# The causal mask of twelve attention groups: a TensorE product into the transposed scores, or a GpSimd selection of the exponentials

## The chip, the cores and the metric

One core of a Trainium2 chip. The metric is the device time of one execution, in microseconds (us), as the median of several runs. The kernel is one program that runs five engines side by side: TensorE (PE in the profile, its weight loads PEld), VectorE (DVE), ScalarE (ACT), GpSimd (POOL) and the queue that issues most transfers (SP).

## The reference, cut to what matters

Four layers over x of 1024 tokens by 256 features, each x + attention(norm(x)) + feed-forward(norm(x)). Layer 0 has a latent attention with 16 heads (rotary and plain features) and beside it a second attention over a shared key; layer 2 has a plain one with 16 heads. All three are causal, and the part that matters here is the same in each:

```python
scores = jnp.einsum('bhtd,bhsd->bhts', q, k) * scale       # layer 0 also adds the rotary product
causal = jnp.tril(jnp.ones((t, t), dtype=bool))
scores = jnp.where(causal[None, None], scores, jnp.float32(-jnp.inf))
attn = jax.nn.softmax(scores, axis=-1)
out = jnp.einsum('bhts,bhsd->bhtd', attn, v)
```

Layer 1 has one causal head over 1024 tokens, layer 3 a running sum in place of attention. The layers' other halves are gated products and aren't touched.

## The kernel before, in words

Heads are taken in 12 groups of four (`GH`): groups 0, 2, 4, 6 are the latent ones of layer 0 (`is_mla`), 1, 3, 5, 7 the ones with a shared key (`is_shared`), 8 to 11 those of layer 2. `GROUPS` holds the two runs, 0 to 7 and 8 to 11. Each group walks over the 8 key tiles (`kt`, 128 keys each).

**Scores (`score_units`, `scores_T`, L1956 to L1985).** For a key tile the scores are computed transposed: 128 keys on the partitions, queries along the columns, from the key tile's first query (`kt * P`) to 1024, in products of at most 512 columns. For kt 0 to 3 a unit is one head in two halves; for kt 4 to 7 it is two heads, one half each. A latent group needs two products for each half: L1962 (`Kr2`, `Qr2`, 128 rows) and L1963 (`Kr`, `Qr`, 113 rows), both 4-byte. The other groups need only L1963, 97 rows of bf16 parts. The last row of the stacks adds minus the row maximum. Each unit goes into one of two halves of `psA` (`a_unit` waits until ScalarE has read the unit before last).

**Exponentials (L1100, L1105).** ScalarE reads each unit out of `psA` through Exp into `Pr` and counts `a_drained`. `Pr` holds two key tiles (places s % 2).

**Selections (`mask_exponentials`, L930 to L936).** When all units of a key tile are drained, GpSimd sets to zero, in place, what lies above the diagonal in the 128 x 128 block of each of the four heads, in one instruction over 512 columns, and counts `masked`.

**Values (`values_product`, L1987 to L2004).** TensorE waits for `masked`, and multiplies the exponentials by the values into `psO`, four heads side by side in 32-column strips. It runs one key tile behind the scores: it is issued after the second unit (and, for kt 0 to 3, the third) of the next key tile (L2098).

**Maxima (`maxima_unit`, L1930 to L1948; VectorE L1420).** The row maxima of the next group are found from untransposed scores in `psD` (two banks; `d_unit` waits until VectorE has read the unit before last). These already carry a mask: behind a product whose block holds the diagonal comes `identb` x `maskq` into its last 128 columns (L1947). When all are reduced, VectorE forms the negated maxima, TensorE transposes them (L1953), and a transfer puts them into the stack as the row of the next group.

**The order of TensorE's work.** It is written by a planner, `paced` with its class `Pace` (L117 to L209): it keeps a clock for each engine in TensorE columns, and after each score unit or values product it takes as many waiting units (maxima, rotary products, selected keys, down weights) as find a free bank, or as the share of the group that has passed asks for. Two of its costs concern the change: `points_of` (the columns of a score unit) and `MASKED`, 1900, after which a key tile's exponentials count as ready for the values product; `HANDOVER` is 480.

**GpSimd's other work between the selections** (L953 to L966): rotary sums, splits of a query tile into bf16 parts, eight-way butterflies of a weight in group 6, and in the last group low parts of expert weights (L1010).

**`scores_T` already has a `mask` argument**, which the layer-1 attention uses (L2275): in the diagonal half it adds `identb` x `maskk` to the first 128 columns (L1965), where `maskk` is 0 where the query may see the key and -1e30 elsewhere, in bf16.

Of the kernel before, what the change touches and what calls it, by code (L numbers as in the profile page):

```python
# [7 lines left out]
ALU = mybir.AluOpType  # L8
# [3 lines left out]
P = 128  # L12
T, D = 1024, 256
NT, DC = T // P, D // P
HALF = 512
H, HD, RD, LAT = 16, 16, 64, 64
GH = 4
# [56 lines left out]
def is_mla(i):  # L74

    return i < 2 * NG and i % 2 == 0
# [34 lines left out]


READ, EXPONENTIAL = (368, 2.5), (400, 2)
MASKED, HANDOVER, SHORT = 1900, 480, 600


class Pace:  # L117


    def __init__(self):  # L120
        self.pe = self.dve = self.act = 0
        self.read, self.copied, self.masked = [0, 0], [0, 0], {}

    def bank_free(self):
        return self.read[-2] <= self.pe + SHORT
# [9 lines left out]
        self.copied.append(self.act)  # L135

    def values(self, columns, s):
        self.pe = max(self.pe, self.masked[s]) + columns


def points_of(groups, i, kt):

    heads = GH if kt < NT // 2 else GH // 2
    points = []
    for k in range(heads):
        points.append(("scores", (T - kt * P) * (1 if kt < NT // 2 else 2) * (2 if is_mla(i) else 1)))
        if (i, kt) != (groups[0], 0) and k in (1, 2):
            columns, b = 0, (kt - 1) % NT
            for half in (0, 1) if heads == 2 else (k - 1,):
                if b * P < (half + 1) * HALF:  # L150
                    columns += HANDOVER + 4 * ((half + 1) * HALF - max(b * P, half * HALF))
            points.append(("values", columns))
    return points


def paced(groups):

    pace, plan, waiting, due, passed = Pace(), {}, {}, {}, {}
    for g in groups[1:]:
        waiting[g], passed[g] = list(MAX_UNITS), 0  # L160
        due[g] = sum(columns for place in max_window(g, groups[0]) for _, columns in points_of(groups, *place))

    def maxima(j, part, h0, nh, w):
        pace.unit(nh * w + (nh * P if part == (j >= NT // 2) else 0), nh * w)

    for i in groups:
        for kt in range(NT):
            g = next((g for g in (i + 1, i + 2) if g in groups and (i, kt) in max_window(g, groups[0])), None)
            products = beside_products(i, kt)
            row = i + 1 in groups and kt == max_end(i + 1)  # L170
            points = points_of(groups, i, kt)
            if (i, kt) == (0, KEY_KT):
                pace.pe += 8 * T
            if (i, kt) == (2 * NG - 1, NT // 2 - 1):
                pace.pe += 8 * T
            plan[i, kt] = (g, [])
            for n, (what, columns) in enumerate(points):
                if what == "scores":
                    pace.scores(columns, (T - kt * P) * (1 if kt < NT // 2 else 2))
                else:  # L180
                    pace.values(columns, NT * i + kt - 1)
                if row and n == 1:
                    pace.pe = max(pace.pe, pace.read[-1] + 2 * HANDOVER)
                    pace.unit(4 * P, P)
                at = []
                behind = 0
                if g is not None:
                    passed[g] += columns
                    behind = len(waiting[g]) - len(MAX_UNITS) * (due[g] - passed[g]) // due[g]
                while (products or waiting.get(g)) and not (row and n == 0):  # L190
                    if not pace.bank_free() and (n < len(points) - 1 if products else len(at) >= behind):
                        break
                    at.append(products.pop(0) if products else waiting[g].pop(0))
                    if at[-1][0] == "rope":
                        pace.unit(2 * HALF, HALF)
                    elif at[-1][0] == "wdn":
                        pace.unit(4 * HALF, HALF, 2)
                    elif at[-1][0] == "kv":
                        pace.unit(8 * HALF, 3 * HALF, 2)
                    else:  # L200
                        maxima(*at[-1])
                plan[i, kt][1].append(at)
            pace.masked[NT * i + kt] = pace.act + MASKED
            if kt == 1 and i - 1 in groups:
                for _ in range(2):
                    pace.unit(16 * P, HALF + (0 if is_mla(i - 1) else 2 * HALF), 2)
            if i == 2 * NG - 1 and kt >= NT // 2:
                pace.unit(8 * HALF, HALF)
    return plan  # L209
# [11 lines left out]
def build(nc, ins, out):  # L221
    with ExitStack() as ctx:
# [380 lines left out]
        stack_in = [sem(f"stack_in{n}") for n in range(4)]  # L603
        part0_cut, keys_masked, head_ready = sem("part0_cut"), sem("keys_masked"), sem("head_ready")
        max_ready, mrow_in = sem("max_ready"), sem("mrow_in")
        pv_done, masked = sem("pv_done"), sem("masked")
        butterflies, had_ready, ones1_ready = sem("butterflies"), sem("had_ready"), sem("ones1_ready")
        se_args, se_ready, comb_ready, comb_out = (
            sem(n) for n in ("se_args", "se_ready", "comb_ready", "comb_out"))
# [234 lines left out]
        def _(pool):  # L844
# [82 lines left out]
            nope_rest(1)  # L927
            nope_rest(3)

            def mask_exponentials(i, kt):  # L930

                s = NT * i + kt
                pool.wait_ge(a_drained, scored(i, kt))
                block_ = Pr[:, (s % 2) * GH * T:(s % 2 + 1) * GH * T].rearrange("p (h t) -> p h t", h=GH)[:, :, tile_cols(kt)]
                pool.affine_select(out=block_, in_=block_, pattern=[[0, GH], [1, P]], compare_op=ALU.is_ge, fill=0.0,  # L935
                                   base=0, channel_multiplier=-1).then_inc(masked, 1)  # L936

            STEPS_AT = (0, 4, 8, 12, 13, 14, 14, 14, 14)  # L940
            steps_1 = [(s, q, op) for s in range(3) for q in range(0, FC, 2 << s) for op in (ALU.add, ALU.subtract)]

# [9 lines left out]

            for i in GROUPS[0]:  # L953
                for kt in range(NT):
                    mask_exponentials(i, kt)
                    if (i, kt) in ROPE_AT:
                        rope_add(ROPE_AT[i, kt])
                    if (i, kt - 1) in ROPE_AT:
                        rope_rest(ROPE_AT[i, kt - 1])
                    if i == 1 and kt < 4:  # L960
                        split_step(1, kt)
                    if i == 6:
                        if kt == 0:
                            pool.wait_ge(w1_in, 16 * N_W1)
                        for step in steps_1[STEPS_AT[kt]:STEPS_AT[kt + 1]]:
                            butterfly(*step)  # L966
# [39 lines left out]

            for i in GROUPS[2]:
                for kt in range(NT):
                    mask_exponentials(i, kt)
                    if i == LAST and kt in (1, 2, 3):  # L1010
                        piece_low(kt - 1)
            for e in range(E):
# [823 lines left out]
        def _(pe):  # L1836
# [131 lines left out]
            def score_units(i, kt):  # L1968

                rows = MLA_ONE + 1 if is_mla(i) else STACK + 1  # L1970

                def one(heads):
                    dst = a_unit()
                    for b, h in enumerate(heads):
                        second = (Kr2[:, tile_cols(kt)], lambda lo, hi: Qr2[:, h * T + lo:h * T + hi]) if is_mla(i) else None
                        k = key_rows(i, h, rows, kt * P, (kt + 1) * P)
                        q = lambda lo, hi: head_rows(Qs, i, h, rows, lo, hi)
                        if len(heads) == 1:
                            for half in range(2):
                                op = scores_T(dst, half * HALF, k, q, kt, half, second)  # L1980
                        else:
                            op = scores_T(dst, b * HALF, k, q, kt, 1, second)
                    op.then_inc(a_filled, 1)
                step = 1 if kt < NT // 2 else 2
                return [list(range(h, h + step)) for h in range(0, GH, step)], one  # L1985

            def values_product(i, kt, halves):  # L1987

                s = NT * i + kt
                pe.wait_ge(masked, s + 1)  # L1990
                if kt == 0 and i > 0:
                    pe.wait_ge(o_drained, i)
                for half in halves:
                    if kt * P >= (half + 1) * HALF:
                        continue
                    lo, hi = max(kt * P, half * HALF), (half + 1) * HALF
                    last_kt = hi // P - 1
                    for h in range(GH):
                        e = Pr[:, ((s % 2) * GH + h) * T + lo:((s % 2) * GH + h) * T + hi]
                        op = pe.matmul(psO[h * VW:(h + 1) * VW, lo:hi], values(i, kt, h), e,  # L2000
                                       start=kt == 0, stop=kt == last_kt, tile_position=(0, h * VW),
                                       skip_group_check=True)
                if 1 in halves:
                    op.then_inc(pv_done, 1)  # L2004
# [467 lines left out]
```

## Time and profile before

| | |
|---|---|
| median of 3 runs | 916.07 us (912.64 to 919.23) |
| the profiled execution: time, span | 915.74 us, 914.0 us |
| busy: TensorE products, VectorE, ScalarE, GpSimd | 824.8, 563.4, 388.4, 238.4 us |
| mean granted TensorE clock | 0.967 of 2.4 GHz |
| selections: number, busy | 96, 61.0 us |

The profile is of one execution. Products of TensorE are pipelined, and their recorded durations include that pipeline, so the busy time of TensorE is more than the time it needs. "The chain of waits" follows the work that ended last back from the end: at each step to what released it, or to the instruction before it on its engine. A releaser is inferred; "issue" is time in which an engine waited for nothing that is recorded. Idle time of an engine counts only where the chain passes.

### The profile page before, as it was taken

How to read it: one execution, taken by the hardware profiler on the slowest of the kernel's cores; microseconds unless marked ns; L12 is line 12 of the kernel's file. 1: busy time of each engine (PE TensorE's matmuls, PEld its weight loads, DVE VectorE, ACT ScalarE, POOL GpSimd, SP SyncE). 2: the span in 40 equal slices, each digit the busy share in tenths (PEclk: the TensorE clock that was granted, in tenths of full speed). 3: DMA queues.
4: the chain of work that ended last, by engine and by line, in shares of the span. 5: the costliest groups of instructions: out<-in, count | busy, mean ns of one | idle time of the engine just before them, and what ended most of it. 6: DMA issues, size and time to landing. Idle time of an engine off the chain costs nothing.

```text
span 914.0 us, 12060 instructions
## 1 busy us (share of the span) xinstructions
PE 824.8 (90%) x4833; PEld 491.4 (54%) x4835; DVE 563.4 (62%) x1000; ACT 388.4 (42%) x481; POOL 238.4 (26%) x215
## 2 busy tenths in 40 slices
PE   8989999899899999996899997858999889989997
PEld 3554553454355435444478793523343248888776
DVE  4987657784876678216543454848776545965552
ACT  3731454446444545563423403134554854510240
POOL 4641222421132114513322101501111236720110
PEclk9989999999999999998989998979999999999999
DMA  6473169416532850204000003779000052000001
GB/s 190 87 245 72 47 146 145 116 47 110 99 82 79 135 141 1 79 1 141 22 1 1 1 1 130 146 120 118 2 2 1 3 195 94 0 1 1 1 0 47
DMA packets 35585, 64.99 MB, mean 71 GB/s; under 512 B 6165, under 2 KB 14909, under 8 KB 35461
## 3 DMA queue, kind: packets, MB, share of 16 engines
q1 hardware_dynamic: 34952, 64.08, 30.1%
q8 instruction: 38, 0.62, 0.3%
q10 hardware_dynamic: 576, 0.13, 0.1%
q14 instruction: 19, 0.15, 0.1%
HBM read 44.35 MB, written 16.29 MB: 66 GB/s over the span
## 4 chain that ended last, share of the span: by engine, by line
PE 66%; DVE 18%; ACT 6%; issue 3%; SPq 3%; POOL 2%; DMA 2%; ACTq 0%; DVEq 0%; POOLq 0%
PE psD L1860 12%; PE psO L2000 11%; PE psA L1860 10%; PE psD L1945 9%; PE psA L1963 8%; DVE mx L1420 8%; PE psO L1860 7%; PE psA L1962 3%; SPq L627 3%; ACT Pr L1100 2%; PE psD L1947 2%; DVE hid_low L1756 1%; PE psD L2014 1%; PE psA L1893 1%; DVE Qs L1541 1%
## 5 line engine op out<-in xcount | busy, mean ns | idle before, releaser
L1420 DVE TENSOR_REDUCE mx<-psD 128x1 f32<-128x512 f32 (+3 forms) x419 | 259.3, 657 | 95.8 <-PE psD L1947 70.5
L1100 ACT ACTIVATE Pr<-psA 128x1024 f32<-128x1024 f32 (+3 forms) x192 | 161.7, 865 | 174.7 <-PE psA L1963 174.3
L935 POOL TENSOR_SCALAR_AFFINE_SELECT Pr<-Pr 128x512 f32<-128x512 f32 x96 | 61.0, 635 | 372.1 <-ACT Pr L1100 296.6
L1105 ACT ACTIVATE Pr<-psA 128x1024 f32<-128x1024 f32 (+3 forms) x96 | 63.6, 703 | 59.9 <-PE psA L1963 59.7
L2000 PE MATMUL psO<-Pr,Vh 128*32 128x512 f32 (+3 forms) x768 | 80.8, 500 | 3.1 <-POOL Pr L935 2.6
L1962 PE MATMUL psA<-Qr,Kr 128*128 128x512 f32 (+3 forms) x192 | 74.7, 403 | 0.7 <-ACT xnT L1045 0.7
L1947 PE MATMUL psD<-maskq,identb 128*128 128x128 bf16 x354 | 70.5, 224 | 0.1
L1963 PE MATMUL psA<-Qr,Kr 113*128 113x512 f32 (+3 forms) x192 | 65.5, 347 | 0.0
L1945 PE MATMUL psD<-Kg,Qs 96*128 96x512 bf16 (+3 forms) x192 | 54.5, 332 | 7.8 <-DVE mx L1420 4.9
L1963 PE MATMUL psA<-Qs,Ks 97*128 97x512 bf16 (+3 forms) x192 | 46.3, 334 | 12.3 <-issue 8.3
L1945 PE MATMUL psD<-Kr,Qr 80*128 80x512 bf16 (+3 forms) x166 | 50.8, 348 | 7.0 <-DVE mx L1420 6.1
L1963 PE MATMUL psA<-Qs,Kg 97*128 97x512 bf16 (+3 forms) x192 | 44.5, 326 | 3.5 <-ACT Pr L1100 1.5
L1962 PEld LDWEIGHTS psA<-Qr,Kr 128*128 128x128 f32 x192 | 36.6, 191 | 18.1 <-ACT Pr L1105 8.4
L1945 PE MATMUL psD<-Ks,Qs 96*128 96x512 bf16 (+3 forms) x144 | 42.8, 342 | 3.6 <-DVE mx L1420 2.8
L1945 PEld LDWEIGHTS psD<-Kg,Qs 96*128 96x128 bf16 x192 | 17.7, 97 | 52.5 <-DVE mx L1420 38.9
L1945 PEld LDWEIGHTS psD<-Kr,Qr 80*128 80x128 bf16 x166 | 16.3, 101 | 45.6 <-DVE mx L1420 37.9
L2000 PE MATMUL psO<-Pr,Vg 128*32 128x512 f32 (+3 forms) x384 | 40.1, 497 | 0.7 <-POOL Pr L935 0.2
L1963 PEld LDWEIGHTS psA<-Qr,Kr 113*128 113x128 f32 x192 | 36.6, 190 | 2.9 <-issue 0.7
L1947 PEld LDWEIGHTS psD<-maskq,identb 128*128 128x128 bf16 x354 | 35.5, 100 | 4.4 <-issue 1.5
L1945 PEld LDWEIGHTS psD<-Ks,Qs 96*128 96x128 bf16 x144 | 13.8, 100 | 39.5 <-DVE mx L1420 34.3
L1534 DVE TENSOR_TENSOR x<-x,psD 128x512 f32<-128x512 f32 x11 | 7.6, 687 | 43.3 <-PE psD L1860 35.9
L1963 PEld LDWEIGHTS psA<-Qs,Ks 97*128 97x128 bf16 x192 | 15.3, 100 | 33.4 <-issue 11.4
(433 smaller groups left out, 1696.3 us busy)
## 6 DMA issues: line engine op xcount, KB each, us to landing
Qr<-d_qr SPq DMA_DIRECT2D x18, 512.0 KB, 12.3
d_qr<-WB SPq DMA_DIRECT2D x9, 512.0 KB, 3.2
Pr<-d_cb SPq DMA_DIRECT2D x8, 512.0 KB, 7.7
Qs<-d_gq SPq DMA_DIRECT2D x24, 128.0 KB, 4.1
Qs<-d_q SPq DMA_DIRECT2D x24, 128.0 KB
Ks<-d_k SPq DMA_DIRECT2D x24, 128.0 KB
Qr<-d_qn SPq DMA_DIRECT2D x18, 128.0 KB, 7.3
Kr<-d_kn SPq DMA_DIRECT2D x18, 128.0 KB, 7.9
```

What stands on the lines that cost most here:

```text
L627: sp.dma_start(dst, src).then_inc(s, 16)
L935: pool.affine_select(out=block_, in_=block_, pattern=[[0, GH], [1, P]], compare_op=ALU.is_ge, fill=0.0, base=0, channel_multiplier=-1).the ...
L1100: act.activation(place[:, h, q0:T], src[:, q0:T], ACT.Exp, scale=score_scale(i)).then_inc(a_drained, 1)
L1105: act.activation(place[:, h:h + 2, q0:T], src[:, :, q0 - HALF:HALF], ACT.Exp, scale=score_scale(i)).then_inc(a_drained, 1)
L1420: dve.tensor_reduce(mx[:, j, part, h0:h0 + nh], src, AX, ALU.max).then_inc(d_drained, 1)
L1541: dve.tensor_tensor(dst[:, c], src[0:r, :], gate_rows[:, c], ALU.mult).then_inc(d_drained, 1)
L1860: op = pe.matmul(dst, lhsT, rhs, start=start and k == 0, stop=stop and k == len(terms) - 1)
L1945: op = pe.matmul(dst[:, k * w:(k + 1) * w], q, kk, start=True, stop=not diagonal)
L1947: op = pe.matmul(dst[:, (k + 1) * w - P:(k + 1) * w], identb[:], maskq[:], start=False, stop=True)
L1962: pe.matmul(out_, second[0], second[1](lo, (half + 1) * HALF), start=True, stop=False)
L1963: op = pe.matmul(out_, k, q(lo, (half + 1) * HALF), start=second is None, stop=not (diagonal and mask))
L2000: op = pe.matmul(psO[h * VW:(h + 1) * VW, lo:hi], values(i, kt, h), e, start=kt == 0, stop=kt == last_kt, tile_position=(0, h * VW), skip_ ...
```

## The change

GpSimd's selections and their semaphore go. `scores_T` is called with `mask=True` in the twelve groups, so that each diagonal half gets a product more (L1965). The values product waits for ScalarE's last exponential of the key tile in place of the selection. The planner counts the columns of the mask products, and takes exponentials as ready `HANDOVER` after ScalarE.

```diff
@@ -111,7 +111,7 @@
 
 
 READ, EXPONENTIAL = (368, 2.5), (400, 2)
-MASKED, HANDOVER, SHORT = 1900, 480, 600
+HANDOVER, SHORT = 480, 600
 
 
 class Pace:
@@ -119,7 +119,7 @@
 
     def __init__(self):
         self.pe = self.dve = self.act = 0
-        self.read, self.copied, self.masked = [0, 0], [0, 0], {}
+        self.read, self.copied, self.ready = [0, 0], [0, 0], {}
 
     def bank_free(self):
         return self.read[-2] <= self.pe + SHORT
@@ -135,7 +135,7 @@
         self.copied.append(self.act)
 
     def values(self, columns, s):
-        self.pe = max(self.pe, self.masked[s]) + columns
+        self.pe = max(self.pe, self.ready[s]) + columns
 
 
 def points_of(groups, i, kt):
@@ -143,7 +143,7 @@
     heads = GH if kt < NT // 2 else GH // 2
     points = []
     for k in range(heads):
-        points.append(("scores", (T - kt * P) * (1 if kt < NT // 2 else 2) * (2 if is_mla(i) else 1)))
+        points.append(("scores", ((T - kt * P) * (2 if is_mla(i) else 1) + P) * (1 if kt < NT // 2 else 2)))
         if (i, kt) != (groups[0], 0) and k in (1, 2):
             columns, b = 0, (kt - 1) % NT
             for half in (0, 1) if heads == 2 else (k - 1,):
@@ -200,7 +200,7 @@
                     else:
                         maxima(*at[-1])
                 plan[i, kt][1].append(at)
-            pace.masked[NT * i + kt] = pace.act + MASKED
+            pace.ready[NT * i + kt] = pace.act + HANDOVER
             if kt == 1 and i - 1 in groups:
                 for _ in range(2):
                     pace.unit(16 * P, HALF + (0 if is_mla(i - 1) else 2 * HALF), 2)
@@ -603,7 +603,7 @@
         stack_in = [sem(f"stack_in{n}") for n in range(4)]
         part0_cut, keys_masked, head_ready = sem("part0_cut"), sem("keys_masked"), sem("head_ready")
         max_ready, mrow_in = sem("max_ready"), sem("mrow_in")
-        pv_done, masked = sem("pv_done"), sem("masked")
+        pv_done = sem("pv_done")
         butterflies, had_ready, ones1_ready = sem("butterflies"), sem("had_ready"), sem("ones1_ready")
         se_args, se_ready, comb_ready, comb_out = (
             sem(n) for n in ("se_args", "se_ready", "comb_ready", "comb_out"))
@@ -927,16 +927,6 @@
             nope_rest(1)
             nope_rest(3)
 
-            def mask_exponentials(i, kt):
-
-                s = NT * i + kt
-                pool.wait_ge(a_drained, scored(i, kt))
-                block_ = Pr[:, (s % 2) * GH * T:(s % 2 + 1) * GH * T].rearrange("p (h t) -> p h t", h=GH)[:, :, tile_cols(kt)]
-                pool.affine_select(out=block_, in_=block_, pattern=[[0, GH], [1, P]], compare_op=ALU.is_ge, fill=0.0,
-                                   base=0, channel_multiplier=-1).then_inc(masked, 1)
-
-
-
             STEPS_AT = (0, 4, 8, 12, 13, 14, 14, 14, 14)
             steps_1 = [(s, q, op) for s in range(3) for q in range(0, FC, 2 << s) for op in (ALU.add, ALU.subtract)]
 
@@ -952,7 +942,6 @@
 
             for i in GROUPS[0]:
                 for kt in range(NT):
-                    mask_exponentials(i, kt)
                     if (i, kt) in ROPE_AT:
                         rope_add(ROPE_AT[i, kt])
                     if (i, kt - 1) in ROPE_AT:
@@ -1006,7 +995,6 @@
 
             for i in GROUPS[2]:
                 for kt in range(NT):
-                    mask_exponentials(i, kt)
                     if i == LAST and kt in (1, 2, 3):
                         piece_low(kt - 1)
             for e in range(E):
@@ -1977,9 +1965,9 @@
                         q = lambda lo, hi: head_rows(Qs, i, h, rows, lo, hi)
                         if len(heads) == 1:
                             for half in range(2):
-                                op = scores_T(dst, half * HALF, k, q, kt, half, second)
+                                op = scores_T(dst, half * HALF, k, q, kt, half, second, mask=True)
                         else:
-                            op = scores_T(dst, b * HALF, k, q, kt, 1, second)
+                            op = scores_T(dst, b * HALF, k, q, kt, 1, second, mask=True)
                     op.then_inc(a_filled, 1)
                 step = 1 if kt < NT // 2 else 2
                 return [list(range(h, h + step)) for h in range(0, GH, step)], one
@@ -1987,7 +1975,7 @@
             def values_product(i, kt, halves):
 
                 s = NT * i + kt
-                pe.wait_ge(masked, s + 1)
+                pe.wait_ge(a_drained, scored(i, kt))
                 if kt == 0 and i > 0:
                     pe.wait_ge(o_drained, i)
                 for half in halves:
```

## Rows read from the trace of the kernel before

**Rows 1.** Page, busy us by engine; clock granted in 40 slices

```profile
PE 824.8 (90%) x4833; PEld 491.4 (54%) x4835; DVE 563.4 (62%) x1000; ACT 388.4 (42%) x481; POOL 238.4 (26%) x215
...
PEclk9989999999999999998989998979999999999999
```

**Rows 2.** Timeline, PE: bf16 products of 128 columns behind one another

```profile
145.61 0.22 PE L1945 MATMUL psD<-Kr,Qr 80*128 80x128 bf16 x1
145.67 0.22 PE L1947 MATMUL psD<-maskq,identb 128*128 128x128 bf16 x1
145.73 0.22 PE L1945 MATMUL psD<-Kr,Qr 80*128 80x128 bf16 x1
```

**Rows 3.** Page and chain of waits, shares of the span

```profile
PE 66%; DVE 18%; ACT 6%; issue 3%; SPq 3%; POOL 2%; DMA 2%; ACTq 0%; DVEq 0%; POOLq 0%
...
by line: PE psD L1860 11.6%; PE psO L2000 10.7%; PE psA L1860 10.1%; PE psD L1945 9.2%; PE psA L1963 8.0%; DVE mx L1420 7.6%; PE psO L1860 7.1%; PE psA L1962 3.4%; issue 3.0%; SPq L627 2.6%; ACT Pr L1100 2.0%; PE psD L1947 1.9%; DVE hid_low
```

**Rows 4.** Waits: engine, line waited for, us in total, times, longest

```profile
ACT Pr L1100 <- PE psA L1963: 174.3, 128, 10.0
PEld psD L1945 <- DVE mx L1420: 112.7, 220, 1.9
...
PEld psD L1953 <- DVE mneg L1425: 9.6, 8, 2.6
```

**Rows 5.** Line 935, the selections: number, ns, who waited for them

```profile
L935 POOL TENSOR_SCALAR_AFFINE_SELECT Pr<-Pr x96: 627/634/688, 84.3 to 740.4; 128x512 f32<-128x512 f32 x96
...
  PEld psO L2000: 11.3, 23
  PE psO L2000: 2.8, 7
  PEld psA L1963: 1.3, 1
```

**Rows 6.** Timeline, PE: values products that waited for a selection

```profile
376.37 0.85 PE L2000 MATMUL psO<-Pr,Vh 128*32 128x384 f32 x8 [0.58 <-POOL Pr L935]
...
712.95 0.64 PE L2000 MATMUL psO<-Pr,Vh 128*32 128x256 f32 x8 [0.42 <-POOL Pr L935]
...
741.12 0.43 PE L2000 MATMUL psO<-Pr,Vh 128*32 128x128 f32 x8 [0.83 <-POOL Pr L935]
```

**Rows 7.** Timeline, PE: products of 128 columns with f32 weights

```profile
131.55 0.27 PE L1962 MATMUL psA<-Qr,Kr 128*128 128x128 f32 x1
...
131.66 0.27 PE L1963 MATMUL psA<-Qr,Kr 113*128 113x128 f32 x1
```

**Rows 8.** Chain of waits, pieces in order of time: start us, us, what

```profile
184.11 0.18 PE psA L1962
...
184.47 0.24 PE psA L1962
...
189.20 0.06 PE psD L1947
```

**Rows 9.** Page, the score products: count, busy us, mean ns, idle before

```profile
L1962 PE MATMUL psA<-Qr,Kr 128*128 128x512 f32 (+3 forms) x192 | 74.7, 403 | 0.7 <-ACT xnT L1045 0.7
...
L1963 PE MATMUL psA<-Qr,Kr 113*128 113x512 f32 (+3 forms) x192 | 65.5, 347 | 0.0
...
L1963 PE MATMUL psA<-Qs,Ks 97*128 97x512 bf16 (+3 forms) x192 | 46.3, 334 | 12.3 <-issue 8.3
...
L1963 PE MATMUL psA<-Qs,Kg 97*128 97x512 bf16 (+3 forms) x192 | 44.5, 326 | 3.5 <-ACT Pr L1100 1.5
```

**Rows 10.** Chain of waits, a bf16 group: products of 512 and 256 columns

```profile
147.68 0.33 PE psA L1963 x2
```

**Rows 11.** Groups by line and form, VectorE: busy us, mean ns

```profile
L1420 DVE TENSOR_REDUCE mx<-psD 128x1 f32<-128x512 f32 x262 | 169.8, 685 | 36.2 <-PE psD L1945 21.9 <-PE psD L1947 13.3 <-DVE xn L1450 0.2
...
L1756 DVE TENSOR_TENSOR hid_low<-Qs,hid_high 128x1024 fp32r<-128x1024 f32 x8 | 15.3, 1908 | 0.0
...
L1666 DVE TENSOR_TENSOR hid_low<-Qs,hid_high 128x1024 fp32r<-128x1024 f32 x8 | 9.6, 1217 | 0.0
```

## What the change will do to the time: the prediction

> **What bounds the kernel now.** I read the page's busy table first, then the chain of waits, then the list of waits, then the timeline around single products. The table has TensorE busy 90% of the span, VectorE 62%, GpSimd only 26%, and TensorE's clock at full speed through nearly all of it [rows 1]. Busy TensorE time is padded: a product of 128 columns is written down as 0.22 us while the next starts 0.06 us later [rows 2]. So I take the bound from the chain. It runs 66% over TensorE, 18% over VectorE and 2% over GpSimd; the two lines of the transposed scores hold 8.0% (L1963) and 3.4% (L1962) of it, the maxima reductions of VectorE 7.6% [rows 3]. The attention stages alternate: TensorE fills a bank and goes on; the next bank it wants is still being reduced by VectorE (220 waits, 112.7 us on the weight-load side), and ScalarE waits 174.3 us for score products [rows 4]. The last shows that ScalarE has time to spare and that score products are what it lacks. GpSimd's 96 selections take 0.634 us each, 61 us in all, but TensorE was held by them for only 11.3 + 1.3 us on its load side and 2.8 us on its product side [rows 5]. The engine that is being relieved is thus nearly free, and the work goes to the one that holds most of the chain.
>
> **What is removed.** 96 selections and the wait on them before each values product. The wait that replaces it (last exponential of the same key tile) is met in advance: the values products come behind the second score unit of the next key tile, and that unit could only start once this same exponential had left its bank. So nothing new is late there. Worth: the seven waits in which products really stood still are 2.8 us [rows 5], three of them being 0.58, 0.42 and 0.83 us [rows 6]. A product's record runs 0.22 us where its successor starts after 0.06 [rows 2], so each such gap is really about 0.16 us longer: 2.8 + 7 x 0.16 = 3.9 us. The other 16 or so load-side waits lie below that padding; I allow 0.6 us. Gain 4.5 us. Its ends: 2.8 us from the product side alone, and 11.3 + 2.8 + 1.3 = 15.4 us if every wait of either side were worth its full length.
>
> **What is added.** Each score product of the diagonal half gets one more: 12 groups x 8 key tiles x 4 heads = 384 products of 128 columns, bf16, each with its own load of the identity. The maxima already do exactly this in VectorE's banks: product and mask follow each other at 145.61, 145.67, 145.73 us, that is 0.06 us each, load hidden [rows 2]; a mask on the chain holds the same (189.20) [rows 8]. In the eight groups with bf16 stacks the price is 0.06 us. In the four latent groups the product behind a mask often needs an f32 load. Such products of 128 columns stand 0.11 us apart (131.55, 131.66), where bf16 ones stand 0.06 apart [rows 2, 7]: the f32 load, which a product of 512 columns covered, sticks out from behind a mask. Of a latent group's 32 masks, those followed by L1962 inside their unit (16 in the first four key tiles, 8 in the last four) cost 0.11, except the 4 + 2 whose own product has 128 columns, where the load was already out in the open (0.06). So 18 x 0.11 + 14 x 0.06 = 2.8 us a group, 0.088 us a mask. In all: 4 x 2.8 + 256 x 0.06 = 26.6 us of TensorE time.
>
> **How much of it is on the path.** A chain step that was late stays late, so masks behind products on the chain lengthen it in full; masks that TensorE runs while VectorE is reducing cost nothing. The share follows from time on the chain over time in all. In a latent group the 24 products of 512 columns take 0.24 us, the 8 of 384 0.18 [rows 8], the 8 of 256 about 0.12 (in proportion) and the 8 of 128 0.11 [rows 7]: 9.1 us, 36.3 in four groups. The chain has 3.4% x 914 = 31.1 us of L1962: 86%. L1963 comes in the same 192 latent products and in 2 x 192 of bf16 [rows 9]; 8.0% x 914 = 73.1 us, less 31.1 for the latent ones (same sizes, same places) and some 2 for the layer-1 scores, leaves 40. A 512 and a 256 in bf16 take 0.33 us together [rows 10], so a group has 24 x 0.22 + 8 x 0.17 + 8 x 0.11 + 8 x 0.06 = 8.0 us, eight groups 64: 62%. Masks on the chain: 128 x 0.86 = 110 at 0.088 us = 9.7 us, and 256 x 0.62 = 159 at 0.06 = 9.5 us. Sum 19.2 us. The bounds are none of the bf16 half absorbed or all of it: from 9.7 to 26.6 us.
>
> The Trainium skill (TensorE: Matmul & The Clock Gate, Back-to-back issue gap) says that a stream of load and product pairs of 128 columns sustains about 81 ns each, against this change. An estimate by it is 269 x 0.081 = 22 us on the chain instead of 19.2. The trace's alternating pairs disagree at 0.06 us [rows 2], and I stay with them.
>
> **What moves.** The planner that spreads the maxima over the score units changes two numbers: 128 more columns for each head, and exponentials ready 480 instead of 1900 columns after ScalarE, 0.6 us sooner at 2.4 GHz. Both are small against a unit, so some maxima move by one place. I take 0 for it. What a move can cost or give is read from VectorE: a reduction of 0.685 us [rows 11] finished too late or in time, once in each of 11 hand-overs between groups: 7.5 us either way. GpSimd's other work (rope sums, butterflies, low parts) comes out from behind the selections, but nothing on the chain waits for it apart from what is counted above. VectorE could gain if GpSimd had been in its way: the same 128 x 1024 subtraction takes 1908 ns in one stage and 1217 in another [rows 11], but the reductions, which are the bulk of its attention work, hold 685 ns; I take 0, and bound it at 2 us.
>
> **Sum.** 914.0 - 4.5 + 19.2 = 928.7 us span; the profiled execution took 915.74 us beside it, so 930.4. That execution stands 0.3 below the median of 916.07. I say 930.
>
> **The rivals.**
> A. Not slower: TensorE's slack takes the masks. Place: the 220 waits for VectorE's banks, half a microsecond each [rows 4]. If the new order puts score units, then 0.06 to 0.17 us longer, into these waits, only the latent groups' 9.7 us remain, and with most of the 15.4 us of selection waits coming back (say 9) the time is 915.74 + 9.7 - 9 = 916. Pushed further (a reduction in time at each hand-over, -7.5) it is 909. For it: the slack is there. Against it: 62% of the bf16 score products are on the chain already, in the order of now. It decides from the point at which under a fifth of the masks stay on the path.
> B. Slower by more: the shift of maxima goes the wrong way. The last maxima of a group come late, and TensorE stands before the transposing product (eight waits now, 9.6 us [rows 4]). All 26.6 us count and 7.5 come on top, with the 2.8 us gain: 915.74 + 26.6 + 7.5 - 2.8 = 947. Half of it gives 939.
> C. The change doesn't relieve GpSimd's followers at all, because the seven waits turn into waits for ScalarE: 915.74 + 19.2 = 935. It is inside the forecast's own range.
>
> **How the numbers follow.** Forecast (with C) 0.62, A 0.25, B 0.13. Forecast's own range 922 to 937. The range that leaves out two in ten reaches into A as far as 914 and into B as far as 940. A measurement of this kernel tells about 1% (9.2 us) from no change. Slower by over that, above 925.2: four fifths of the forecast's case, and B: 0.62. Within: the rest of the forecast's case and most of A: 0.28. Faster: the far end of A: 0.10.
>
> **What would show it.** Right: a new group at L1965 with 384 + 8 products, starting 0.06 us behind their product in bf16 groups and followed at 0.11 in latent ones; L935 gone; GpSimd busy near 238 - 61 = 177 us; values products no longer waiting for GpSimd; each group of attention 1 to 2.5 us longer; the chain with about 16 to 20 us of L1965. Wrong: VectorE's share of the chain falling by ten microseconds or more (A), or a wait before the transposing product several microseconds longer (B), or mask products at 0.08 us and over.

## The result, and the profile after

The changed kernel took 927.68 us in the median (922.37 to 928.75, 4 runs) beside 914.36 us for the kernel before (4 runs): ratio 1.0107, 95% interval 1.0064 to 1.015. A second comparison on one chip (8 runs against 25) gave 1.0091, 1.0061 to 1.0121. Slower by 5.6 to 13.7 us, then. The profiled execution is the fastest of its four, with a span of 920.6 us.

The page of the changed kernel: busy times, granted clock, and the shares of the chain.

```profile
PE 850.1 (92%) x5217; PEld 511.8 (56%) x5219; DVE 560.3 (61%) x1000; ACT 390.3 (42%) x481; POOL 177.3 (19%) x119
...
PEclk9989999999999999998889998989999999999999
...
PE 73%; DVE 17%; ACT 5%; issue 2%; DMA 1%; POOL 1%; SPq 0%; DVEq 0%; ACTq 0%; POOLq 0%
...
L1950 PE MATMUL psA<-Qr,Kr 128*128 128x512 f32 (+3 forms) x192 | 84.6, 441 | 0.7 <-ACT xnT L1033 0.7
L1953 PE MATMUL psA<-maskk,identb 128*128 128x128 bf16 x392 | 84.6, 225 | 0.0
```

Against [rows 1] GpSimd has lost 61 us, and TensorE has gained 25. The mask products are there, 392 with the eight of layer 1, at L1953 now. The row to stop at is L1950, the old L1962 [rows 9]: it does the same 192 products, and its busy time has risen from 74.7 to 84.6 us.

The waits of the changed kernel (in total, times, longest), and its chain by line:

```profile
PEld psD L1933 <- DVE mx L1408: 94.1, 196, 1.2
```

```profile
by line: PE psD L1848 11.9%; PE psO L1988 11.2%; PE psA L1848 11.0%; PE psD L1933 10.0%; PE psA L1951 9.4%; DVE mx L1408 7.4%; PE psO L1848 7.1%; PE psA L1950 4.6%; PE psA L1953 2.1%; issue 2.1%; PE psD L1935 2.1%; ACT Pr L1088 1.5%; DVE hi
```

No wait for a selection is left. Those of the values products' loads have become shorter waits for ScalarE, which weren't there before, while the products themselves wait neither for a selection nor for an exponential any more:

```profile
PEld psO L1988 <- ACT Pr L1088: 4.5, 18, 0.4
PEld psO L1988 <- ACT Pr L1093: 4.4, 18, 0.5
```

Waits for VectorE's banks have fallen from 112.7 to 94.1 us [rows 4]; experiments 4, 8 and 9 tell which masks went into them. L1953 holds 2.1% x 920.6 = 19.3 us of the chain.

**A finer ruler.** One execution differs from the next by several microseconds, but not everywhere. VectorE copies out each group's row of maxima once (a cast to `mrowb` in the groups with bf16 stacks, to `mrow` in the latent ones), while the group before it is at its fifth or sixth key tile. In the middle of layer 0 the stretch from one shared group's row to the next one's holds a shared and a latent group's worth of work, 32 masks of each kind. Where the same code was profiled twice, this stretch agreed within 0.1 us. In the kernel before, from group 3's row to group 5's:

```profile
210.49 0.28 DVE L1438 CAST mrowb<-psD 32x128 bf16<-32x128 f32 x1 [3.09 <-PE psD L1953]
...
294.20 0.28 DVE L1438 CAST mrowb<-psD 32x128 bf16<-32x128 f32 x1 [3.09 <-PE psD L1953]
```

and in the changed kernel:

```profile
210.23 0.28 DVE L1426 CAST mrowb<-psD 32x128 bf16<-32x128 f32 x1 [4.36 <-PE psD L1941]
...
296.67 0.28 DVE L1426 CAST mrowb<-psD 32x128 bf16<-32x128 f32 x1 [4.36 <-PE psD L1941]
```

83.71 us before, 86.44 after: a pair of groups costs 2.7 us more. (The second profile of the changed kernel has 86.46; experiment 12, whose code is that of before up to the last group, has 83.69.) This "pair" is the ruler of the experiments. It isn't the same everywhere, so a longer one stands beside it: from group 2's row to group 7's, 204.75 us before and 212.56 after, again within 0.1 us for the same code. TensorE's granted clock is 1.00 in both stretches in every profile.

What differs between executions lies elsewhere: ahead of group 1's row, after attention, from group 10's row to group 11's, where the mean clock of the stretch is between 0.88 and 0.96 (it takes 39.2 us at 0.96 and 40.9 at 0.92 in the two profiles of the changed kernel), and where the first group of layer 2 waits for its row's transfer. There TensorE stood 8.27 us in the profile of before and 4.72 us in that of the change, which is 3.5 us of why the two spans differ by only 6.6:

```profile
607.84 1.01 PE L1963 MATMUL psA<-Qs,Ks 97*128 97x512 bf16 x2 [8.27 <-issue]
```

```profile
611.75 0.58 PE L1951 MATMUL psA<-Qs,Ks 97*128 97x512 bf16 x1 [4.72 <-issue]
```

### The profile page after: what moved, and what is told of

The parts are those of the page before. It is cut to its first block, busy times and chain, and to the rows that moved or that the text cites. A ratio compares the mean times of both kernels' runs of the same rounds, so it can differ in the third digit from the quotient of the medians.

```text
span 920.6 us, 12725 instructions
## 1 busy us (share of the span) xinstructions
PE 850.1 (92%) x5217; PEld 511.8 (56%) x5219; DVE 560.3 (61%) x1000; ACT 390.3 (42%) x481; POOL 177.3 (19%) x119
## 4 chain that ended last, share of the span: by engine, by line
PE 73%; DVE 17%; ACT 5%; issue 2%; DMA 1%; POOL 1%; SPq 0%; DVEq 0%; ACTq 0%; POOLq 0%
PE psD L1848 12%; PE psO L1988 11%; PE psA L1848 11%; PE psD L1933 10%; PE psA L1951 9%; DVE mx L1408 7%; PE psO L1848 7%; PE psA L1950 5%; PE psA L1953 2%; PE psD L1935 2%; ACT Pr L1088 2%; DVE hid_low L1744 1%; PE psD L2002 1%; DVE xn L1368 1%; DVE Qs L1529 1%
## 5 line engine op out<-in xcount | busy, mean ns | idle before, releaser
L1950 PE MATMUL psA<-Qr,Kr 128*128 128x512 f32 (+3 forms) x192 | 84.6, 441 | 0.7 <-ACT xnT L1033 0.7
L1953 PE MATMUL psA<-maskk,identb 128*128 128x128 bf16 x392 | 84.6, 225 | 0.0
L1951 PE MATMUL psA<-Qs,Ks 97*128 97x512 bf16 (+3 forms) x192 | 52.6, 336 | 8.5 <-issue 4.7
L1951 PE MATMUL psA<-Qs,Kg 97*128 97x512 bf16 (+3 forms) x192 | 50.9, 327 | 2.2 <-ACT Pr L1088 1.2
L1953 PEld LDWEIGHTS psA<-maskk,identb 128*128 128x128 bf16 x392 | 38.5, 98 | 23.4 <-issue 15.2
L1950 PEld LDWEIGHTS psA<-Qr,Kr 128*128 128x128 f32 x192 | 37.9, 197 | 16.5 <-ACT Pr L1093 8.4
L1933 PEld LDWEIGHTS psD<-Kr,Qr 80*128 80x128 bf16 x166 | 16.1, 100 | 38.2 <-DVE mx L1408 31.8
L1951 PEld LDWEIGHTS psA<-Qs,Ks 97*128 97x128 bf16 x192 | 18.7, 99 | 31.8 <-ACT Pr L1088 10.3
L993 POOL TENSOR_TENSOR egu_low<-WA,pieces_k 128x512 fp32r<-128x512 f32 x6 | 7.7, 1280 | 136.2 <-ACT pieces_k L1063 136.2
## 6 DMA issues: line engine op xcount, KB each, us to landing
Qr<-d_qr SPq DMA_DIRECT2D x18, 512.0 KB, 11.6
```

What stands on the lines that cost most here:

```text
L1933: op = pe.matmul(dst[:, k * w:(k + 1) * w], q, kk, start=True, stop=not diagonal)
L1950: pe.matmul(out_, second[0], second[1](lo, (half + 1) * HALF), start=True, stop=False)
L1951: op = pe.matmul(out_, k, q(lo, (half + 1) * HALF), start=second is None, stop=not (diagonal and mask))
L1953: op = pe.matmul(out_[:, 0:P], identb[:], maskk[:], start=False, stop=True)
```

## The experiments

My theory: the masks on the chain are the cost (19 us), the selections were worth 4.5, the order nothing. Rivals: the planner's new order is part of it; slack takes the masks; the selections were worth far more.

**1. The change beside its parts.** No edit.

> The changed kernel itself, beside the runs that take it apart, on the same chip. Both theories expect what was measured before: ratio to the kernel before 1.006 to 1.015.

Measured: ratio 1.0091 (1.0061 to 1.0121), 927.14 us against 917.61.

**2. Masks in the order of before.** Edit to the changed kernel:

```diff
-HANDOVER, SHORT = 480, 600
+MASKED, HANDOVER, SHORT = 1900, 480, 600
-        points.append(("scores", ((T - kt * P) * (2 if is_mla(i) else 1) + P) * (1 if kt < NT // 2 else 2)))
+        points.append(("scores", (T - kt * P) * (1 if kt < NT // 2 else 2) * (2 if is_mla(i) else 1)))
-            pace.ready[NT * i + kt] = pace.act + HANDOVER
+            pace.ready[NT * i + kt] = pace.act + MASKED
```

> The change with the planner's two numbers as they were (1900 and no mask columns). My theory (the order moves little, the masks on the chain are the cost): within 2 us of the changed kernel. Rival (the planner's new order is part of the cost, or of what softens it): 4 us or more away from the changed kernel, on either side.

Measured: ratio 1.0139 (1.0105 to 1.0173), 931.78 us. That is 4.6 us slower than the change, at the rival's mark. The pair:

```profile
213.46 0.28 DVE L1426 CAST mrowb<-psD 32x128 bf16<-32x128 f32 x1 [3.50 <-PE psD L1941]
...
301.04 0.28 DVE L1426 CAST mrowb<-psD 32x128 bf16<-32x128 f32 x1 [3.50 <-PE psD L1941]
```

87.58 us, 1.1 more than the change. So the order isn't worth nothing: in the pair the new one takes back a quarter of the 4.0 us that masks cost in the old order. How much it is in all is less sure. The two ratios lie 0.5% apart, with an uncertainty of nearly as much. The longer ruler has 2.3 us less with the new order, the stretch from group 9's row to group 10's 0.4 more, so what can be read of it in the trace is some 2 us.

**3. Neither selections nor masks, order of before.** Experiment 2 with `mask=True` taken out of both calls in `score_units`.

> No selections and no masks, order of before: layers 0 and 2 attend without a causal mask. What it saves against the kernel before is the whole worth of the selections. My theory: 4.5 us (ratio 0.995). Rival (most waits for GpSimd count): 10 us or more (ratio 0.989 or less).

Measured: ratio 0.9955 (0.993 to 0.998), 914.23 us: 4.1 us for all selections, as worked out. The pair is 83.54 us, only 0.2 less than before; little is to be had in the middle. A gain lies where TensorE has no maxima to go on with, as in the last stretch, from the row of group 11 to the last copy of the outputs: 31.8 us before, 30.7 here. In this one profile, though, the granted clock averaged 0.95 there, where it is 1.00 in all others. At 1.00 the stretch takes 30.0 us with neither (experiment 4) and 31.8 with selections (experiment 5), in the order of the change. So the selections are worth 1.8 us there. The interval of all selections is 1.8 to 6.4 us.

**4. Neither, order of the change.**

> No selections and no masks, order of the change (layers 0 and 2 attend without a causal mask). The changed kernel minus this is the cost of 384 mask products in place. My theory: 19 us between the two, so a ratio of about 0.99 to 0.995 to the kernel before. Rival (slack takes half the masks): 10 us or less between the two. Second rival (all count): 26 us.

Measured: ratio 0.9933 (0.9907 to 0.9959), 912.87 us. The masks cost 1.0091 - 0.9933 = 1.6%, or 14.5 us, in the order of the change, and 1.0139 - 0.9955 = 1.8%, or 16.9 us, in the order of before. Forecast 19.2; between the first rival's 10 and my 19. The pair:

```profile
210.46 0.28 DVE L1426 CAST mrowb<-psD 32x128 bf16<-32x128 f32 x1 [3.83 <-PE psD L1941]
...
293.54 0.28 DVE L1426 CAST mrowb<-psD 32x128 bf16<-32x128 f32 x1 [3.83 <-PE psD L1941]
```

83.08 us. All masks of a pair cost 86.45 - 83.08 = 3.4 us, those between the rows of groups 2 and 7 (156 masks) 212.6 - 203.6 = 9.0 us. The 14.5 us for all has an uncertainty of about 4 us.

**5. Selections in the order of the change.** The kernel before with the planner's two lines of the change.

> The kernel before with only the planner's two numbers of the change: selections stay, no masks. The order was worth about 4 us beside masks and 2 us without either. If the order is simply better: 2 to 4 us faster than before (ratio 0.996 to 0.998). Rival (the old 1900 was there for the selections, which the new order puts on the path): 2 us or more slower than before, with the waits for GpSimd up from 11.3 us.

Measured: ratio 1.0019 (0.9992 to 1.0047). The pair is 83.16 us, 0.5 less, and the longer ruler 1.0 less, but from group 9's row to group 10's it is 0.5 more; the waits for GpSimd are as they were (11.4 us), and the median doesn't show a gain. The rival fails by its own mark, and the forecast of 2 to 4 us faster does too: alone, the order isn't worth a measurable amount.

**6. Each mask twice.** `for again in range(2)` around the mask product in the twelve groups.

> The change with each mask product of the twelve groups issued twice (384 more products, same result). If a mask costs a fixed share of its 0.06 to 0.11 us (the chain in series): another 23 us of TensorE time (the second one always stands 0.06 behind the first), of which 60 to 75% shows: 14 to 17 us over the change, like the first set. Rival (the first set used up the slack in VectorE's waits): the second set shows in nearly full, 20 us or more.

Measured: ratio 1.0311 (1.0284 to 1.0339), 942.56 us: 20 us over the change by the ratios, 15 by the medians, which come from two chips. The two don't agree well enough to choose between the two expectations. The pair is 88.56 us, another 2.1 for 64 x 0.06 = 3.8 us of products (55%), and the longer ruler 218.10, another 5.5 for 156 x 0.06 = 9.4 us (59%), which speaks for the first in layer 0: the first set had not used up the slack there.

**7. Masks behind the unit.** In `score_units` the mask products of a unit come after its last score product.

```diff
-                if diagonal and mask:
+                if diagonal and late is not None:
+                    late.append(out_[:, 0:P])
+                elif diagonal and mask:
                     op = pe.matmul(out_[:, 0:P], identb[:], maskk[:], start=False, stop=True)
...
+                    for out_ in late:
+                        op = pe.matmul(out_, identb[:], maskk[:], start=False, stop=True)
                     op.then_inc(a_filled, 1)
```

> The change with the mask products of a unit put behind the unit's last score product, so that none stands ahead of an f32 load inside the unit. My theory (18 masks of each latent group pay 0.05 us for that load): 0.9 us less in each latent group, 3.6 us in all, and nothing in the bf16 groups. Rival (the load isn't what costs, the masks' own time is): within 1 us of the change in the latent groups too.

Measured: ratio 1.0101 (1.0067 to 1.0135), which can't be told from the change. The pair is 85.50 us, 0.95 less, as expected in size. That it comes from the latent group follows from elsewhere: the layer-2 stretches, which have bf16 masks only, don't change (34.19 for 34.24, 31.1 for 31.2), and the busy time of L1950 falls from 84.6 back to 75.9 us. The longer ruler is 2.9 us shorter, too much for the rival. What it shows besides is the price of one mask inside a unit. The chain of the changed kernel, start and us of each piece:

```profile
184.90 0.18 PE psA L1950
185.08 0.18 PE psA L1951
185.26 0.07 PE psA L1953
185.34 0.32 PE psA L1950
185.65 0.24 PE psA L1951
```

and with the masks behind the unit:

```profile
184.46 0.17 PE psA L1950
184.63 0.18 PE psA L1951
184.81 0.24 PE psA L1950
185.05 0.24 PE psA L1951
185.29 0.07 PE psA L1974
```

A product of 512 columns takes 0.24 us, as in [rows 8]. Behind a mask it takes 0.32 (0.29 in most places). With its own 0.07 such a mask costs 0.12 to 0.15 us, not the 0.11 of my sum. This is where L1950's busy time came from. The weight loads (PEld) of the kernel before and of the changed one show what the product waits for:

```profile
184.13 0.19 PEld L1962 LDWEIGHTS psA<-Qr,Kr 128*128 128x128 f32 x1
...
185.10 0.10 PEld L1953 LDWEIGHTS psA<-maskk,identb 128*128 128x128 bf16 x1 [0.17 <-issue]
185.10 0.20 PEld L1950 LDWEIGHTS psA<-Qr,Kr 128*128 128x128 f32 x1
```

Before, this load of 0.19 us ran beside the product of 384 columns ahead of it, which started at 184.13 too and holds 0.18 us. After, the load starts with the mask product (185.10), which holds only 0.07. The price stood in the trace of before as well, where a maxima mask comes ahead of a latent group's score product:

```profile
339.85 0.06 PE psD L1947
339.91 0.29 PE psA L1962
```

**8. Masks in the latent groups only.** `mask=is_mla(i)` in both calls.

> Order of the change, no selections, masks in the four latent groups only (the other eight attend without a causal mask). Against the kernel with neither it shows the latent groups' part of the 14.5 us that all masks cost. My theory (chain share 86% at 0.088 us against 62% at 0.06): half of it, 7 to 9 us, some 2.2 us in each latent group. Rival (masks cost the same anywhere): a third of it, 5 us.

Measured: ratio 1.0082 (1.005 to 1.0115). The pair:

```profile
210.19 0.28 DVE L1426 CAST mrowb<-psD 32x128 bf16<-32x128 f32 x1 [4.36 <-PE psD L1941]
...
296.16 0.28 DVE L1426 CAST mrowb<-psD 32x128 bf16<-32x128 f32 x1 [4.36 <-PE psD L1941]
```

85.97 us. The latent group's 32 masks cost 2.9 of the 3.4 us; I expected 2.2. By the ratios it is 1.0082 - 0.9933 = 1.5%, more than my 7 to 9 us, but this difference has an uncertainty of 4 us, and four times 2.9 is 11.6. Not every latent group pays the same: from group 5's row to group 7's the same masks cost 80.11 - 76.46 = 3.65 us. On the longer ruler 84 latent masks cost 8.2 us, 0.098 us each.

**9. Masks in the bf16 groups only.** `mask=not is_mla(i)`.

> Order of the change, no selections, masks in the eight bf16 groups only (the four latent ones attend without a causal mask). Stretches between row hand-overs repeat to 0.1 us, and by them a latent and a shared group together take 83.1 us with no mask, 86.0 with latent masks only, 86.45 with all. If the two kinds add up (bf16 masks of layer 0 are mostly absorbed beside VectorE): 83.4 to 83.8 us, a quarter of their 1.9 us. Rival (the first masks to come are absorbed, whichever they are, and the slack is shared): 82.9 to 83.2, nothing at all. My prediction's share of 62% would be 84.3.

Measured: ratio 0.9998 (0.9965 to 1.003). The pair:

```profile
208.25 0.28 DVE L1426 CAST mrowb<-psD 32x128 bf16<-32x128 f32 x1 [3.84 <-PE psD L1941]
...
291.85 0.28 DVE L1426 CAST mrowb<-psD 32x128 bf16<-32x128 f32 x1 [3.82 <-PE psD L1941]
```

83.60 us, 0.5 for the shared group's 32 masks, a quarter of their 1.9 us. 0.5 and 2.9 make the 3.4 of both: the two kinds add up, and the rival of a shared slack falls. On the longer ruler 72 shared masks cost 1.1 us, which with the 8.2 is within 0.4 of the 9.0 of both. The slack is VectorE's, as its waits over the whole kernel show: with neither kind (experiment 4), with the bf16 masks only, and with the latent masks only (experiment 8):

```profile
PEld psD L1933 <- DVE mx L1408: 113.2, 232, 1.7
...
PEld psD L1933 <- DVE mx L1408: 96.9, 203, 1.1
...
PEld psD L1933 <- DVE mx L1408: 109.9, 224, 1.4
```

The bf16 masks, 256 x 0.06 = 15.4 us of products, take 16.3 us off these waits, the latent ones 3.3. In layer 2 the same bf16 masks cost more: the stretch from the row of group 9 to that of group 10 takes 33.2 us without masks and 34.2 with them, half of their 1.9 us, and the last stretch 30.0 and 31.2, half of the 2.4 us of its 40 masks.

**10 and 11. One planner number at a time**, each a single execution.

> The change, with only one of the planner's numbers new: exponentials ready after 480, mask columns not counted. The pair of a latent and a shared group took 87.5 us with both numbers old and 86.45 with both new. If readiness is what helps: 86.5. If the columns are: 87.5.

> The change, with only the other number new: mask columns counted, exponentials ready after 1900. If the columns are what helps: 86.5 us for the pair. If readiness is: 87.5.

Measured: the pair takes 87.66 us with only the readiness new and 86.47 with only the columns. The columns are what helps; the 1900 of the selections did no harm. The waits of the weight loads for VectorE's banks sum to 93.7 us in experiment 1 and in experiment 2 alike. But those of the products themselves, in which TensorE really stood still, are fewer and shorter with the new placing of the maxima. In experiment 2 and in experiment 1:

```profile
PE psD L1933 <- DVE mx L1408: 11.0, 27, 0.9
...
PE psD L1933 <- DVE mx L1408: 7.1, 19, 0.6
```

They are 11.6 us with only the readiness new and 7.1 with only the columns. So the placing helps by bringing fewer products to a bank that is still being reduced.

**12. TensorE masks in the last group only**, selections elsewhere, order of before:

```diff
-                pe.wait_ge(masked, s + 1)
+                if i == LAST:
+                    pe.wait_ge(a_drained, scored(i, kt))
+                else:
+                    pe.wait_ge(masked, s + 1)
```

with `mask=i == LAST` in both calls, and no selection in that group.

> The kernel before, with TensorE masks in place of the selections in the last group alone, where TensorE stood longest for GpSimd and ScalarE holds the chain. The last stretch takes 31.8 us before, 31.2 with masks, 30.7 with neither. Expected: 0.6 us less in that stretch, paid with up to 1 us at the group's start where maxima don't fill it; total within the measurement of the kernel before (0.997 to 1.001). Rival (GpSimd's waits at the end are worth their length, 4 to 5 us in the last group): ratio 0.995.

Measured: ratio 0.9979 (0.9956 to 1.0002), 915.04 us against 917.05. The loads' waits for GpSimd fall from 11.3 to 6.8 us, and the last stretch from 31.8 to 31.4 us:

```profile
PEld psO L2004 <- POOL Pr L935: 6.8, 17, 0.8
```

4.5 us of waits away, 0.4 us of time back in that stretch. This is a balance: by experiments 4, 5 and 9 the selections were worth 1.8 us there and the masks cost 1.2. That 1.8 is near the 2.0 us of the product side's five waits in that stretch and far from the 5.4 us of the load side's. It may be the best of the versions that compute the whole layer, but the interval reaches 1, so that isn't shown.

**All stretches.** In us, from one profile each (two for the change), between the rows of the groups named; "last" is from group 11's row to the last copy of the outputs.

| kernel | row 3 to 5 (pair) | row 2 to 7 | row 9 to 10 | last |
|---|---|---|---|---|
| before | 83.71 | 204.75 | 32.73 | 31.8 |
| the change | 86.44, 86.46 | 212.56, 212.57 | 34.24, 34.23 | 31.2, 31.2 |
| 2, masks, order of before | 87.58 | 214.91 | 33.84 | 31.2 |
| 3, neither, order of before | 83.54 | 204.38 | 32.72 | 30.7 (clock 0.95) |
| 4, neither, order of the change | 83.08 | 203.57 | 33.23 | 30.0 |
| 5, selections, order of the change | 83.16 | 203.74 | 33.23 | 31.8 |
| 6, each mask twice | 88.56 | 218.10 | 35.40 | 32.5 |
| 7, masks behind the unit | 85.50 | 209.64 | 34.19 | 31.1 |
| 8, latent masks only | 85.97 | 211.76 | 33.24 | 30.0 |
| 9, bf16 masks only | 83.60 | 204.71 | 34.24 | 31.2 |
| 10, only the readiness new | 87.66 | 215.04 | 33.84 | 31.2 |
| 11, only the columns new | 86.47 | 212.64 | 34.24 | 31.2 |
| 12, masks in the last group | 83.69 | 204.64 | 32.73 | 31.4 |

## Why the prediction was right, and where its terms were off

The sum said 930, and the comparisons give 8 to 13 us slower for its 14.7. What bounds the kernel and what the change trades were right. That the sum came so near is in part luck: the two terms of the masks were off in opposite directions, and the order was put at nothing.

- **The selections' worth (4.5 us): right.** Experiment 3 measures 4.1 (1.8 to 6.4); 1.8 of it lies in the last stretch, 0.4 between the rows of groups 2 and 7, and the rest wasn't located. The wait list of 15 us would have misled; the seven waits of the product side [rows 5] were the right ones to count.
- **The bound: right.** GpSimd's busy time fell by 61 us as forecast (177 us), and the kernel became slower.
- **The latent masks (9.7 us): the mechanism right, the price too small.** I took 0.11 us for a mask ahead of an f32 load, from products of 128 columns that follow each other [rows 7]. It is 0.12 to 0.15 (experiment 7). Experiment 8 has 2.9 us in one pair and 3.65 in the next where I had 0.86 x 2.8 = 2.4, and 8.2 us on the longer ruler where my terms give 84 x 0.86 x 0.088 = 6.4. The share of 86% was too low as well.
- **The bf16 masks (9.5 us): the share was too large for layer 0.** The chain held 62% of these score products by my count, but their masks cost a quarter in the shared groups and half in layer 2 (experiment 9). On the longer ruler that is 1.1 us where my terms give 72 x 0.62 x 0.06 = 2.7. Both kinds together come to 9.0 us there, and my terms to 9.0 too: 1.8 us too little for one kind and 1.5 too much for the other. I had one average over eight groups, which differ by two. The likely reason, by the waits of experiment 9, is that the mask behind a product on the old chain can take the place of a wait for VectorE, so it needn't cost its time. Why the shared groups absorb more than those of layer 2 was not traced further and stays open.
- **The order (0 us): wrong, by 2 to 4.6 us.** Experiments 2, 10 and 11: the planner's mask columns save 1.1 us in the pair and 2.3 on the longer ruler, and lose 0.4 in layer 2; the medians say 4.6, with an uncertainty of about 4. I had bounded it at 7.5 us either way and taken the middle. With it the sum is 10 to 12.7 us. The lower end lies in both measured intervals, the upper only in that of the first comparison (to 13.7; the second ends at 11.1).
- **The chain after.** It holds 19.3 us of mask products, just what I forecast, yet the masks cost 14.5. The agreement is of two different things (the 14.5 has an uncertainty of 4 us, so the gap is near it): the chain after the change runs through the masks, and past other pieces of the old one (VectorE 17% for 18%). What a new piece holds in the chain afterwards isn't what it cost.
- **The rivals.** A had its mechanism: the waits for VectorE fell by 18.6 us, and the bf16 masks are what went into them (experiment 9), but the latent ones, at nearly full price, kept it from deciding. B did not come: the waits before the transposing product fell, from 9.6 to 6.5 us on the load side. VectorE's own wait for that product grew by 1.3 us (4.36 for 3.09 in the rows above). C came in its mechanism only: the loads' waits for GpSimd became 8.9 us of waits for ScalarE, so the replacing wait wasn't always met in advance, but no product waited for an exponential, and the selections' 4.1 us were had all the same.
- The Trainium skill's 81 ns for a pair of load and product (TensorE: Matmul & The Clock Gate, Back-to-back issue gap) isn't borne out for bf16 masks: on the chain a mask holds 0.06 to 0.07 us. Its rule there that the spacing is set by both operations, the load and the product, fits the f32 loads: 0.29 to 0.32 us behind a mask in place of 0.24.

## What to carry to other kernels

Moving work off an engine that is 26% busy onto the one that holds two thirds of the chain pays only what the waits on the idle engine really held up, here 4 us of 61, and it costs the new work's price in each stage by that stage's own slack: here nearly in full in the latent groups (8.2 us for 84 masks), a half in layer 2 and a quarter in the shared groups. Price a small product with its successor: if the next one loads f32 weights, those come out from behind it. Count the new work in whatever plans the order; that alone gave back a quarter of the masks' cost in the stretches that can be read. And find a stretch of the trace that repeats to 0.1 us from one execution to the next, since it resolves what medians that scatter by 1% can't. Look at its granted clock first, and measure more than one such stretch: the same masks cost 2.9 us in one pair and 3.65 in the next.

## What the runs showed of the hardware

A product of 128 columns hides a bf16 weight load (0.06 us from product to product), but only in part an f32 load: the next product of 512 columns then takes 0.29 to 0.32 us in place of 0.24. The loads themselves are recorded at 0.10 us for bf16 and 0.19 to 0.20 for f32, and the one looked at in experiment 7 started together with the product ahead of its own. In a row of 128-column products with f32 weights they stand 0.11 us apart [rows 7], 0.05 more than bf16 ones; behind a single short product the extra is that 0.05 in most places and 0.08 in some. What makes the difference wasn't found out.

The stretch from group 10's row to group 11's is code that doesn't differ between the kernel before and experiment 12. It took 37.9 us with a mean granted clock of 0.95 in one and 41.1 us with 0.88 in the other: The instruction counts of all engines and the busy times of VectorE and ScalarE (25.8 and 19.5 us) are the same in both, so the 3 us of difference are the clock's.
